# Gated linear attention in chunks of 64 tokens instead of 128, on one NeuronCore of Trainium2

## The chip, the core and the metric

The kernel runs on one NeuronCore of a Trainium2 chip. The metric is the device time of one execution in microseconds. Shown for a kernel are the median of several executions, and one further execution that the hardware profiler recorded.

## What is computed

One transformer block on 8192 tokens of width 512, in fp32. The part that matters here is the gated linear attention with 16 heads of 64 channels:

```python
h = layernorm(x) * (1 + ca) + sa
q, k, v = h @ Wq.T, h @ Wk.T, h @ Wv.T            # [s, 16, 64] each
g = -softplus(h @ Wd.T + bd)                      # [s, 16]
k = k * sigmoid(h @ Wg.T)
s_t = exp(g_t) * s_{t-1} + outer(k_t, v_t)        # per head, 64 x 64
o_t = q_t @ s_t
x = x + ga * ((rmsnorm(o) * norm_w * sigmoid(h @ Wog.T)) @ Wo.T)
```

After it comes a feed-forward part (three products of 512 x 512). The scan over 8192 tokens isn't made token by token: within a chunk of tokens the scores k.q, weighted by the decay between the two tokens and cut to the past, are multiplied with v, and what came before the chunk enters through the 64 x 64 state.

## The kernel before

`prepare` (L69) splits the attention's weights into high and low parts. `attention_pass` (L346) makes o and writes it to HBM. `output_pass` (L976) reads it back and makes the rest. Only the second of these is changed, and in `output_pass` the order in which o is loaded (`load_o`, L1030).

The tokens are cut into 32 tiles of 256 tokens (T), each of two chunks (NC) of 128 (CH). The pass is software-pipelined: in turn i the projections of tile i are made while the attention of tile i-1 is made. A turn has 8 pairs p of heads. Each engine has its program written out by hand, `pe_tile`, `act_tile`, `dve_tile`, `pool_tile` and `sp_tile`, and they meet only in semaphores. Turns 2 to 29 are a loop; 0, 1, 30, 31 and 32 are written out.

For pair p PE does, in this order (L571 to L638):
- two transposes of kg into psX (L581), from which DVE makes kw, the keys weighted by the decay to the chunk's end (L873);
- the projection g of the next tile (`project`, L509: 4 steps of k, each with 3 matmuls of 128 x 128 with 256 moving columns, L55 to L57);
- the attention's matmuls, called the block here: `weigh_v` (L540) with 4 matmuls v.prob of the pair before, 4 matmuls kw.v into psK (L606), 8 scores kg.q into psS (L614), and `add_held` (L552) with 4 matmuls of state.q of the pair before, which add to the sums of `weigh_v` in psO;
- the projections q and k of the next tile. Behind pair 4 come four projections of v; for p = 0 the projection v4 stands before the block and v5 behind it, and behind pair 7 stand g, q and k of the last channels.

All of the block is fp32. An fp32 matmul of the program is two instructions in the profile, and each has a weight load of its own on the row PEld. `weigh_v` and psK use half of the array (128 rows x 64 columns), the scores and `add_held` a quarter (64 x 64):

```python
nc.tensor.matmul(psO[side * DH:(side + 1) * DH, h, :], v[:, c, p * P + h * DH:p * P + (h + 1) * DH],
                 prob[:, p % 2, 2 * h + c, :], start=True, stop=False, tile_position=(0, side * DH))
```

DVE, for each pair: kw (L873), qg (L818), the two steps of the state, mid (L883) and state (L886), each with 64 columns, then the product of prob with the scores (L889, 512 columns), then `gate_k` (L804) for the projection k. Pair 4 adds `norm_stats`, pair 5 the two steps to softplus' input ahead of kw (L862, L866) and g_raw and `norm_x` behind, pair 6 the copy of cum_out (L904). At p = 0 four `rest_h` (L799) end the pair. ACT makes the four exponentials of the decay (L730, 128 columns each), the copy held of the state (L712), the tanh of the gate (L686), the copy of o out of psO (`copy_o`, L717) and the copy of q (L699). POOL cuts the decay rows to the past (`mask_rows`, L943). SP loads the rows (`spread_rows` L424, `grow_rows` L431), stores o (`store_o` L445) and stores cum_out once a turn (L484).

Where PE waits: ahead of `weigh_v` for prob, mid, held, qg and o; ahead of L606 for kw, state, and for q and v (L599 to L602); ahead of the projection k of pair 6 for w_new and o (L629, L631).

Of the kernel before, what the change touches and what calls it, by code (L numbers as in the profile page):

```python
# [23 lines left out]
P = 128  # L24
# [321 lines left out]
def attention_pass(nc, t, W, norm, h_parts, next_jobs, stage, h_next, h_loaded, wmod_v, x_v, o_v, h_v, cum_v, cum_b):  # L346
    with ExitStack() as ctx:
# [3 lines left out]
        def ps(name, shape):  # L351
# [8 lines left out]
        prob = sb("prob", [P, 2, 4, CH])  # L360
# [5 lines left out]
        mid = sb("mid", [P, 2, DH])  # L366
# [7 lines left out]
        w_new = sb("w_new", [P, 4, NC * H])  # L374
        w_cur = sb("w_cur", [P, 3, NC, H])
        w_all = sb("w_all", [P, NC, NP])
# [7 lines left out]
        psS, psX, psK = psB[:, :, 0:2, :], psB[:, 0, 2:4, :], psB[:, 1, 2:4, 0:DH]  # L384
# [4 lines left out]
        psC = psT[:, 1, NC * H:4 * NC * H]  # L389
# [3 lines left out]
                 "m_sum m_read m_out gate cur proj by_act k e mask score prob kT kw inc mid state held qg gla o zero")  # L393
# [29 lines left out]

        def spread_rows(sp, i, p):  # L424
# [24 lines left out]
        def sp_tile(sp, i, gla, proj, prep, opens=False):  # L449
            j = i - 1  # L450
            for p in range(NP):
# [12 lines left out]
                if p == 7 and proj:  # L464
                    sp.wait_ge(s["n_rows"], 16 * (i + 1))
# [43 lines left out]
        def project(i, kind, b, pe, turns_decay=False):  # L509
# [30 lines left out]
        def weigh_v(pe, n, p):  # L540
            pe.wait_ge(s["prob"], n + 1)
            pe.wait_ge(s["mid"], n + 1)
# [3 lines left out]
            for c in range(NC):  # L546
                for h in range(2):
                    side = (h + c) % 2
                    nc.tensor.matmul(psO[side * DH:(side + 1) * DH, h, :], v[:, c, p * P + h * DH:p * P + (h + 1) * DH],
                                     prob[:, p % 2, 2 * h + c, :], start=True, stop=False, tile_position=(0, side * DH))  # L550

        def add_held(pe, p):  # L552
            for c, s_in in enumerate((held, mid)):
                for h in range(2):
                    r, side = slice(h * DH, (h + 1) * DH), (h + c) % 2
                    last = nc.tensor.matmul(psO[side * DH:(side + 1) * DH, h, :], s_in[r, p % 2, :],  # L556
                                            qg[r, p % 2, c * CH:(c + 1) * CH], start=False, stop=True,
                                            tile_position=(h * DH, side * DH))
# [10 lines left out]
        def pe_tile(pe, i, gla, proj, prep, opens=False):  # L569
            j = i - 1  # L570
            for p in range(NP):  # L571
# [11 lines left out]
                if p == 6 and proj:  # L583
                    pe.wait_ge(s["g_raw"], i + 1)
                    pe.wait_ge(s["hT"], KD * (i + 2 if prep else i + 1))
                    for n3, m in enumerate(("upto", "after", "ones")):
                        last = nc.tensor.matmul(psC[:, n3 * NC * H:(n3 + 1) * NC * H], t[m][:, :], g_raw[:, :],
                                                start=True, stop=True)
                    last.then_inc(s["cum"], 1)
                if p == 0 and gla:  # L590
                    project(j, "v", 4, pe)
                if p > 0 and proj:
                    project(i, "g", p - 1, pe)
                if gla:
                    if p > 0 or not opens:
                        if p == 7 and proj:
                            pe.wait_ge(s["n_out"], i + 1)
                        weigh_v(pe, n - 1, (p - 1) % NP)
                    pe.wait_ge(s["kw"], n + 1)  # L599
                    hold(pe, s["state"], n)  # L600
                    pe.wait_ge(s["by_act"], act_done(j, ("q", p)))
                    pe.wait_ge(s["by_act"], act_done(j, ("v", 5 if p > 3 else 3)))  # L602
                    for c in range(NC):
                        for h in range(2):
                            r = slice(h * DH, (h + 1) * DH)
                            last = nc.tensor.matmul(psK[r, c, :], kw[:, c, r],  # L606
                                                    v[:, c, p * P + h * DH:p * P + (h + 1) * DH],
                                                    start=True, stop=True, tile_position=(0, h * DH))
# [9 lines left out]
                    if p > 0 or not opens:  # L618
# [22 lines left out]
        def _(pe):  # L641
# [9 lines left out]
            weigh_v(pe, NP * NT - 1, NP - 1)  # L651
# [49 lines left out]
        def turn_decay(act, i):  # L701
# [3 lines left out]
            nc.scalar.activation(w_new[:, 1:4, :], psC.rearrange("p (a b) -> p a b", a=3),  # L705
# [725 lines left out]
```

## Time and profile before

| | us |
|---|---|
| median of 3 runs (3398.72 to 3400.33) | 3399.99 |
| the profiled execution's own time | 3399.61 |
| its span, first to last instruction | 3397.7 |
| PE busy (share of the span) | 3343.4 (98%) |
| PE weight loads busy | 3067.8 (90%) |
| DVE busy | 1707.5 (50%) |
| ACT busy | 1350.8 (40%) |
| POOL busy | 435.0 (13%) |

The span is the stretch that the profile covers; 1.9 us of the execution's own time lie around it. The shares of busy time are means over stages that differ: the weights are prepared until about 60 us, the attention pass ends at about 2104 us, and the rest is the output pass. The length of a matmul in the trace is from its start to its modelled end, and matmuls overlap, so what a group of them costs is read from the distance of starts, not from their lengths. PE at 98% therefore doesn't say that PE can't be made faster.

### The profile page before, as it was taken

The page shows a single profiled execution, that of the slowest core. Times are in us where ns is not written, and L with a number is a line of the kernel's source. Part 1 is how long each engine was busy: PE and PEld are TensorE (multiplying, and loading weights), DVE is VectorE, ACT ScalarE, POOL GpSimd, SP SyncE. Part 2 cuts the span into 40 slices and gives each one's busy share as a digit, 9 for nine tenths or more (in the row PEclk, how much of TensorE's full clock was granted, in tenths as well). Part 3 has the DMA queues.
Part 4 walks back from the last instruction along what each step waited for, and adds up shares of the span by engine and source line. Part 5 has one row for each costly group of instructions (what it writes and reads, how often), then busy time and mean ns, then how long its engine had stood idle before and what let it go on. Part 6 is the DMA issues. An engine that isn't in the chain of part 4 may idle for free. (4 is left out here: it accounts for less than half of the span.)

```text
span 3397.7 us, 84855 instructions
## 1 busy us (share of the span) xinstructions
PE 3343.4 (98%) x31109; PEld 3067.8 (90%) x31109; DVE 1707.5 (50%) x3988; ACT 1350.8 (40%) x3584; POOL 435.0 (13%) x723
## 2 busy tenths in 40 slices
PE   7999999999999999999999997999999999999998
PEld 6999999999999999999999996889998899999887
DVE  6333333333333333333333334677667766766776
ACT  4444444444444444444444444333333333333332
POOL 0101100111111011011011102111111111211110
PEclk8999999999999999999999999999999999999999
DMA  5232322322322322322322325322233222232320
GB/s 205 90 108 76 102 98 77 109 88 86 106 82 89 106 80 92 105 78 93 105 75 93 102 69 171 94 74 81 79 84 89 74 74 74 79 82 78 92 77 25
DMA packets 233704, 309.17 MB, mean 91 GB/s; under 512 B 16016, under 2 KB 149152, under 8 KB 233648
## 3 DMA queue, kind: packets, MB, share of 16 engines
q1 hardware_dynamic: 231536, 304.20, 28.9%
q10 hardware_dynamic: 2112, 4.19, 0.4%
q8 instruction: 39, 0.64, 0.1%
q14 instruction: 17, 0.14, 0.0%
HBM read 223.40 MB, written 84.93 MB: 91 GB/s over the span
## 5 line engine op out<-in xcount | busy, mean ns | idle before, releaser
L730 ACT ACTIVATE prob<-cum_rows,w_cur 128x128 f32<-128x128 f32 x1024 | 327.8, 395 | 8.9 <-issue 5.2
L883 DVE SCALAR_TENSOR_TENSOR mid<-state,w_all,psB 128x64 f32<-128x64 f32 x256 | 71.9, 281 | 515.6 <-PE psB L614 515.6
L809 DVE SCALAR_TENSOR_TENSOR kg<-gate,psJ 128x256 f32<-128x256 f32 x256 | 107.9, 421 | 403.2 <-PE psJ L57 364.5
L55 PE MATMUL psJ<-h_hi,w_q_hi 128*128 128x256 f32 x1024 | 309.1, 302 | 0.0
L55 PE MATMUL psJ<-h_hi,w_g_hi 128*128 128x256 f32 x1024 | 305.6, 298 | 3.5 <-DVE h_lo L801 3.5
L55 PE MATMUL psG<-h_hi,w_og_hi 128*128 128x256 f32 x1024 | 287.7, 281 | 6.0 <-ACT og L1167 3.1
L55 PE MATMUL psJ<-h_hi,w_k_hi 128*128 128x256 f32 x1024 | 286.8, 280 | 0.7 <-ACT w_new L705 0.7
L56 PE MATMUL psJ<-h_lo,w_g_hi 128*128 128x256 f32 x1024 | 286.2, 280 | 0.0
L56 PE MATMUL psJ<-h_lo,w_q_hi 128*128 128x256 f32 x1024 | 285.7, 279 | 0.0
L57 PE MATMUL psJ<-h_hi,w_g_lo 128*128 128x256 f32 x1024 | 285.7, 279 | 0.0
L57 PE MATMUL psJ<-h_hi,w_q_lo 128*128 128x256 f32 x1024 | 285.4, 279 | 0.0
L56 PE MATMUL psG<-h_lo,w_og_hi 128*128 128x256 f32 x1024 | 284.8, 278 | 0.0
L57 PE MATMUL psG<-h_hi,w_og_lo 128*128 128x256 f32 x1024 | 284.7, 278 | 0.0
L57 PE MATMUL psJ<-h_hi,w_k_lo 128*128 128x256 f32 x1024 | 284.4, 278 | 0.0
L56 PE MATMUL psJ<-h_lo,w_k_hi 128*128 128x256 f32 x1024 | 283.8, 277 | 0.0
L55 PE MATMUL psJ<-w_v_hi,h_hi 128*128 128x264 f32 (+1 forms) x768 | 252.8, 329 | 0.6 <-DVE kg L809 0.6
L56 PE MATMUL psJ<-w_v_lo,h_hi 128*128 128x264 f32 (+1 forms) x768 | 246.3, 321 | 0.0
L57 PE MATMUL psJ<-w_v_hi,h_lo 128*128 128x264 f32 (+1 forms) x768 | 246.1, 320 | 0.0
L717 ACT COPY o<-psP 128x256 f32<-128x256 f32 x256 | 94.8, 370 | 351.3 <-PE psP L556 347.8
L55 PEld LDWEIGHTS psJ<-h_hi,w_q_hi 128*128 128x128 f32 x1024 | 193.3, 189 | 37.3 <-issue 37.3
L1167 ACT ACTIVATE og<-psG 128x512 f32<-128x512 f32 x128 | 76.5, 598 | 356.5 <-PE psG L57 356.5
L699 ACT COPY q<-psJ 128x256 f32<-128x256 f32 x256 | 95.3, 372 | 276.3 <-PE psJ L57 276.3
(231 smaller groups left out, 9551.2 us busy)
## 6 DMA issues: line engine op xcount, KB each, us to landing
cum_rows<-cum_dram SPq DMA_DIRECT2D x256, 256.0 KB, 3.9
grown<-cum_dram SPq DMA_DIRECT2D x256, 128.0 KB
o_dram<-o SPq DMA_DIRECT2D x256, 128.0 KB, 3.3
o_cols<-o_dram SPq DMA_DIRECT2D x128, 256.0 KB, 4.9
an_norm_x<-in_L_attn_x_dram SPq DMA_DIRECT2D x32, 512.0 KB, 5.4
h_dram<-h_hi SPq DMA_DIRECT2D x32, 512.0 KB, 2.7
h_dram<-h_lo SPq DMA_DIRECT2D x32, 512.0 KB, 4.2
h_hi<-h_dram SPq DMA_DIRECT2D x32, 512.0 KB, 4.0
```

The lines of the kernel that those rows point to most:

```text
L55: nc.tensor.matmul(out, w_hi, x_hi, start=first, stop=False)
L56: nc.tensor.matmul(out, w_hi, x_lo, start=False, stop=False)
L57: return nc.tensor.matmul(out, w_lo, x_hi, start=False, stop=last)
L699: nc.scalar.copy(q[:, b, :], psJ[USES.index(("q", b)) % 2][:, 0:T]).then_inc(s["by_act"], 1)
L717: nc.scalar.copy(o[:, p % 2, :, :], psO[:, :, :]).then_inc(s["o"], 1)
L730: last = nc.scalar.activation(prob[:, p % 2, 2 * h + c, :], cum_rows[:, p % 4, 2 * h + c, :], ACT.Exp, bias=w_cur[:, 0, c, 2 * p + h:2 * p ...
L809: nc.vector.scalar_tensor_tensor(out=kg[:, b, :], in0=gate[:, b % 2, :], scalar=1.0, in1=psJ[USES.index(("k", b)) % 2][:, 0:T], op0=ALU.ad ...
L883: nc.vector.scalar_tensor_tensor(out=mid[:, p % 2, :], in0=state[:, p, :], scalar=w_all[:, 0, p:p + 1], in1=psK[:, 0, :], op0=ALU.mult, op ...
L1167: nc.scalar.activation(og[:, n % 2, :, :], psG[n % 2][:, :].rearrange("p (b t) -> p b t", b=2), ACT.Sigmoid).then_inc(s["sg"], 1)
```

## The change

The chunk becomes 64 tokens: a tile of 256 tokens is now four chunks, indexed (c, b) with b the half of a 128-token piece. Every matmul of the block is a quarter of the array with 64 moving columns, 8 of each kind. The state takes four steps for each tile instead of two. The products of prob and v go to psO and those of the state and q to psH, in another part of the same PSUM tensor, and are added outside: ACT copies psH to o, and then DVE adds psO (`sum_o`). PE's waits for the whole block stand ahead of the last three matmuls of the projection before it.

```diff
+        mid = sb("mid", [P, 2, 3, DH])
+        w_new = sb("w_new", [P, 5, NC * H])
+        w_all = sb("w_all", [P, NC, 2, NP])
+        g_half = sb("g_half", [P, 2, NC * H])
+        later = sb("later", [P, DH])
-        psS, psX, psK = psB[:, :, 0:2, :], psB[:, 0, 2:4, :], psB[:, 1, 2:4, 0:DH]
+        psS, psX = psB[:, :, 0, :], psB[:, 0, 2:4, :]
+        psK = psB[:, :, 1, :].rearrange("p b (c d) -> p b c d", c=NC)
+        psH = psP[:, :, 3, :]
...
         def spread_rows(sp, i, p):
             hold(sp, s["e"], NP * i + p - 3)
-            sp.dma_start(cum_rows[:, p % 4, :, :].rearrange("p (h c) t -> p h (c t)", h=2),
-                         cum_b[i, 0, 2 * p:2 * p + 2, :].unsqueeze(0).to_broadcast([P, 2, T])
-                         ).then_inc(spread[p % 4], 16)
+            for b in range(2):
+                sp.dma_start(rows_of(p)[b * DH:(b + 1) * DH, :, :],
+                             cum_b[i, 0, 2 * p:2 * p + 2, b * CH:(b + 1) * CH].unsqueeze(0).to_broadcast([DH, 2, CH])
+                             ).then_inc(spread[p % 4], 16)
...
-                    sp.dma_start(cum_v[i], cum_out[:, :]).then_inc(s["n_rows"], 16)
+                    for b in range(2):
+                        sp.dma_start(cum_v[i, :, b, :, :], cum_out[:, b * DH:(b + 1) * DH]).then_inc(s["n_rows"], 16)
...
+                if ready and k == KD - 1:
+                    ready()
...
-        def weigh_v(pe, n, p):
+        def o_ready(pe, n):
             pe.wait_ge(s["prob"], n + 1)
-            pe.wait_ge(s["mid"], n + 1)
+            pe.wait_ge(s["mid"], 3 * (n + 1))
             pe.wait_ge(s["held"], n + 1)
             pe.wait_ge(s["qg"], n + 1)
             hold(pe, s["o"], n)
+
+        def kv_ready(pe, j, p):
+            n = NP * j + p
+            pe.wait_ge(s["kw"], n + 1)
+            hold(pe, s["state"], n)
+            pe.wait_ge(s["by_act"], act_done(j, ("q", p)))
+            pe.wait_ge(s["by_act"], act_done(j, ("v", 5 if p > 3 else 3)))
+
+        def weigh_v(pe, p):
+            for h in range(2):
+                for b in range(2):
+                    for c in range(NC):
+                        nc.tensor.matmul(psO[c * DH:(c + 1) * DH, b, h * DH:(h + 1) * DH],
+                                         v[b * DH:(b + 1) * DH, c, p * P + h * DH:p * P + (h + 1) * DH],
+                                         prob[b * DH:(b + 1) * DH, p % 2, 2 * h + c, :], start=True, stop=True,
+                                         tile_position=(b * DH, c * DH))
 
         def add_held(pe, p):
+            for b in range(2):
+                for c in range(NC):
+                    for h in range(2):
+                        r = slice(h * DH, (h + 1) * DH)
+                        s_in = mid[r, p % 2, 2 * c + b - 1, :] if c or b else held[r, p % 2, :]
+                        last = nc.tensor.matmul(psH[c * DH:(c + 1) * DH, h, b * DH:(b + 1) * DH], s_in,
+                                                qg[r, p % 2, c * CH + b * DH:c * CH + (b + 1) * DH], start=True, stop=True,
+                                                tile_position=(h * DH, c * DH))
             last.then_inc(s["gla"], 1)
...
+                def ready():
+                    if follows:
+                        if p == 7 and proj:
+                            pe.wait_ge(s["n_out"], i + 1)
+                        o_ready(pe, n - 1)
+                    kv_ready(pe, j, p)
+
+                if p == 0 and gla:
+                    project(j, "v", 4, pe, ready=ready)
+                elif proj and p > 0:
+                    project(i, "g", p - 1, pe, ready=ready if gla else None)
...
+                        for b in range(2):
+                            for h in range(2):
+                                r, rows = slice(h * DH, (h + 1) * DH), slice(b * DH, (b + 1) * DH)
+                                last = nc.tensor.matmul(psK[r, b, c, :], kw[rows, c, r],
+                                                        v[rows, c, p * P + h * DH:p * P + (h + 1) * DH],
+                                                        start=True, stop=True, tile_position=(b * DH, h * DH))
...
-                                last = nc.tensor.matmul(psS[rows, h, c, :], kg[r, p, c * CH + b * DH:c * CH + (b + 1) * DH],
-                                                        q[r, p, c * CH:(c + 1) * CH], start=True, stop=True,
-                                                        tile_position=(h * DH, b * DH))
+                                at = slice(c * CH + b * DH, c * CH + (b + 1) * DH)
+                                last = nc.tensor.matmul(psS[rows, h, c * DH:(c + 1) * DH], kg[r, p, at], q[r, p, at],
+                                                        start=True, stop=True, tile_position=(h * DH, b * DH))
...
         def copy_o(act, n, p, j):
             act.wait_ge(s["gla"], n + 1)
             hold(act, store[p % 2], 16 * (NP // 2 * j + p // 2))
-            nc.scalar.copy(o[:, p % 2, :, :], psO[:, :, :]).then_inc(s["o"], 1)
+            nc.scalar.copy(o[:, p % 2, :, :], psH).then_inc(s["o_part"], 1)
...
+        def sum_o(dve, n, p):
+            dve.wait_ge(s["o_part"], n + 1)
+            nc.vector.tensor_tensor(o[:, p % 2, :, :].rearrange("p h (b t) -> p h b t", b=2),
+                                    o[:, p % 2, :, :].rearrange("p h (b t) -> p h b t", b=2),
+                                    psO.rearrange("p b (h t) -> p h b t", h=2), ALU.add).then_inc(s["o"], 1)
...
+                    for m in range(4):
+                        c, b = m // 2, m % 2
+                        if m:
+                            dve.wait_ge(s["mid"], 3 * n + m)
+                        into, done = (mid[:, p % 2, m, :], s["mid"]) if m < 3 else (state[:, p, :], s["state"])
+                        nc.vector.scalar_tensor_tensor(out=into, in0=mid[:, p % 2, m - 1, :] if m else state[:, p, :],
+                                                       scalar=w_all[:, c, b, p:p + 1], in1=psK[:, b, c, :], op0=ALU.mult,
+                                                       op1=ALU.add).then_inc(done, 1)
                     dve.wait_ge(s["e"], n + 1)
+                    pr = prob[:, p % 2, :, :].rearrange("p (h c) t -> p h (c t)", h=2)
+                    nc.vector.tensor_tensor(pr, pr, psS, ALU.mult).then_inc(s["prob"], 1)
+                if gla and (p > 0 or not opens):
+                    sum_o(dve, n - 1, (p - 1) % NP)
...
+                    for b in range(2):
+                        rows = slice(b * DH, (b + 1) * DH)
+                        nc.vector.tensor_scalar(g_half[rows, b, :].rearrange("p (h c) -> p c h", c=NC), zt[rows, 0, :, :],
+                                                -1.0, None, ALU.mult)
...
+        def mask_rows(pool, i, p):
...
-            nc.gpsimd.affine_select(out=cum_rows[:, p % 4, :, :], in_=cum_rows[:, p % 4, :, :], compare_op=ALU.is_ge,
-                                    fill=fill, base=0, pattern=[[0, 4], [1, CH]],
-                                    channel_multiplier=-1).then_inc(s["mask"], 1)
+            rows = rows_of(p).rearrange("p h (c t) -> p h c t", c=NC)
+            nc.gpsimd.tensor_tensor(rows, rows, later[:, :].unsqueeze(1).unsqueeze(1).to_broadcast([P, 2, NC, DH]),
+                                    ALU.add).then_inc(s["mask"], 1)
```

Not shown: the masks are cut to blocks of 64 once at the start, the exponentials read 64 columns each, the decay's matmul with ones takes g_half with 64 columns, qg is written with its pieces in another order, and `load_o` of the output pass reads the same bytes with four DMAs as before.

## Rows read from the trace of the kernel before

**Rows 1.** View by stages: us, busy time of each engine, clock, DMA share, GB/s
```profile
101.00:2062.50 1961.50, 1959.29 (x22169) 1821.87 (x22170) 735.62 (x2105) 878.17 (x2679) 210.14 (x523) 1.00 0.28 93
2062.50:2104.00 41.50, 27.23 (x324) 19.98 (x322) 26.92 (x53) 24.00 (x57) 12.15 (x22) 0.95 0.65 214
2104.00:3397.70 1293.70, 1279.58 (x8064) 1153.70 (x8064) 889.00 (x1698) 410.28 (x769) 206.51 (x160) 0.99 0.28 77
```

**Rows 2.** Timeline of PE over one pair: start us, length us, instructions
```profile
1000.25 0.28 PE L56 MATMUL psJ<-h_lo,w_g_hi 128*128 128x256 f32 x1
1000.37 0.28 PE L57 MATMUL psJ<-h_hi,w_g_lo 128*128 128x256 f32 x1
1000.58 0.66 PE L549 MATMUL psP<-prob,v 128*64 128x128 f32 x8
1001.06 0.40 PE L606 MATMUL psB<-v,kw 128*64 128x64 f32 x8
1001.39 0.67 PE L614 MATMUL psB<-q,kg 64*64 64x128 f32 x16
1001.88 0.27 PE L556 MATMUL psP<-qg,held 64*64 64x128 f32 x1
1001.89 0.28 PE L556 MATMUL psP<-qg,mid 64*64 64x128 f32 x2
...
1002.00 0.28 PE L556 MATMUL psP<-qg,mid 64*64 64x128 f32 x2
...
1002.21 0.39 PE L55 MATMUL psJ<-h_hi,w_q_hi 128*128 128x256 f32 x1
1002.43 0.28 PE L56 MATMUL psJ<-h_lo,w_q_hi 128*128 128x256 f32 x1
```

**Rows 3.** Groups by form, 300 to 1700 us: busy us, mean ns, idle
```profile
L606 PE MATMUL psB<-v,kw 128*64 128x64 f32 x1432 | 71.8, 221 | 0.0
```

**Rows 4.** View of one line, PE's sequencer: ns min/median/max, first and last start
```profile
L45 PEldq ALU_OP  x2: 32/32/32, 1001.5 to 1001.8; - x2
...
L45 PEldq EVENT_SEMAPHORE  x1: 51/51/51, 2080.9 to 2080.9; - x1
...
L601 PEldq EVENT_SEMAPHORE  x1: 51/51/51, 2081.0 to 2081.0; - x1
```

**Rows 5.** Timeline of DVE, ACT and PE around the same pair
```profile
1002.13 0.28 DVE L883 SCALAR_TENSOR_TENSOR mid<-state,w_all,psB 128x64 f32<-128x64 f32 x1 [1.99 <-PE psB L614]
1002.45 0.28 DVE L886 SCALAR_TENSOR_TENSOR state<-mid,w_all,psB 128x64 f32<-128x64 f32 x1
...
1005.60 0.42 DVE L873 TENSOR_TENSOR kw<-psB,w_cur 128x256 f32<-128x256 f32 x1
...
1002.43 0.37 ACT L717 COPY o<-psP 128x256 f32<-128x256 f32 x1 [0.96 <-PE psP L556]
...
1006.34 0.28 PE L55 MATMUL psJ<-h_hi,w_g_hi 128*128 128x256 f32 x1
```

**Rows 6.** Timeline of DVE and PE at pair 1 of a tile
```profile
1050.35 0.42 DVE L873 TENSOR_TENSOR kw<-psB,w_cur 128x256 f32<-128x256 f32 x1
...
1050.62 0.28 PE L55 MATMUL psJ<-h_hi,w_g_hi 128*128 128x256 f32 x1
```

**Rows 7.** Timeline of DVE and PE at pair 5 of a tile
```profile
1018.20 0.42 DVE L873 TENSOR_TENSOR kw<-psB,w_cur 128x256 f32<-128x256 f32 x1
...
1018.38 0.28 PE L55 MATMUL psJ<-h_hi,w_g_hi 128*128 128x256 f32 x1
```

**Rows 8.** Timeline of PE at pair 6 of a tile
```profile
1025.74 0.66 PE L549 MATMUL psP<-prob,v 128*64 128x128 f32 x8
...
1028.89 0.28 PE L55 MATMUL psJ<-h_hi,w_k_hi 128*128 128x256 f32 x1
```

**Rows 9.** POOL's groups over the whole span, and SP's timeline at a tile's end
```profile
L1322 POOL TENSOR_TENSOR sq<-sq 128x256 f32<-128x256 f32 x32 | 33.9, 1061 | 2.5
...
1032.14 2.07 SPq L427 DMA_DIRECT2D cum_rows<-cum_dram  x4
```

More of the change, by code:

```diff
@@ L359, in attention_pass @@
         o = sb("o", [P, 2, NC, CH])
-        prob = sb("prob", [P, 2, 4, CH])
+        prob = sb("prob", [P, 2, 4, DH])
         g_raw = sb("g_raw", [P, NC * H])
@@ L388, in attention_pass @@
         psT = ps("psT", [P, KD, T])
-        psC = psT[:, 1, NC * H:4 * NC * H]
+        psH = psP[:, :, 3, :]
+        psC = psT[:, 1, NC * H:5 * NC * H]
         psM = psP[:, 1, 2, 0:KD]
         s = signals(nc, ctx, "a", "xT hT h_hi h_lo h_kept zb softin e1 l soft g_raw cum w_new n_turned n_out n_rows "
-                 "m_sum m_read m_out gate cur proj by_act k e mask score prob kT kw inc mid state held qg gla o zero")
+                 "m_sum m_read m_out gate cur proj by_act k e mask score prob kT kw inc mid state held qg gla o_part o zero")
         s.update(norm["s"])
@@ L506, in _, with project @@
             sp.wait_ge(s["h_kept"], 32 * NT)
-        def project(i, kind, b, pe, turns_decay=False):
+        def project(i, kind, b, pe, turns_decay=False, ready=None):
             u = USES.index((kind, b))
@@ L545, in weigh_v @@
             hold(pe, s["o"], n)
[L546 to L550, printed above, removed]
-        def add_held(pe, p):
[L553 to L558, printed above, removed]
+        def kv_ready(pe, j, p):
[12 more added lines that the diff above has]
+                                         tile_position=(b * DH, c * DH))
+        def add_held(pe, p):
+            for b in range(2):
[6 more added lines that the diff above has]
+                                                tile_position=(h * DH, c * DH))
             last.then_inc(s["gla"], 1)
@@ L585, in pe_tile @@
                     pe.wait_ge(s["hT"], KD * (i + 2 if prep else i + 1))
-                    for n3, m in enumerate(("upto", "after", "ones")):
-                        last = nc.tensor.matmul(psC[:, n3 * NC * H:(n3 + 1) * NC * H], t[m][:, :], g_raw[:, :],
-                                                start=True, stop=True)
-                    last.then_inc(s["cum"], 1)
[L590 to L593, printed above, removed]
@@ L594, in pe_tile @@
-                if gla:
-                    if p > 0 or not opens:
+                    for n3, m in enumerate(("upto", "after")):
+                        nc.tensor.matmul(psC[:, n3 * NC * H:(n3 + 1) * NC * H], t[m][:, :], g_raw[:, :],
+                                         start=True, stop=True)
+                    last = nc.tensor.matmul(psC[:, 2 * NC * H:4 * NC * H], t["ones"][:, :],
+                                            g_half[:, :, :].rearrange("p b n -> p (b n)"), start=True, stop=True)
@@ L596, in pe_tile @@
+                    last.then_inc(s["cum"], 1)
+                follows = p > 0 or not opens
+                def ready():
+                    if follows:
                         if p == 7 and proj:
                             pe.wait_ge(s["n_out"], i + 1)
[L598 to L602, printed above, removed]
@@ L603, in pe_tile @@
-                    for c in range(NC):
[L604 to L608, printed above, removed]
+                        o_ready(pe, n - 1)
+                    kv_ready(pe, j, p)
@@ L650, in _ @@
             turn_w(pe, NW - 1)
-            weigh_v(pe, NP * NT - 1, NP - 1)
+            o_ready(pe, NP * NT - 1)
+            weigh_v(pe, NP - 1)
             add_held(pe, NP - 1)
@@ L729, in act_tile @@
                         for h in range(2):
-                            last = nc.scalar.activation(prob[:, p % 2, 2 * h + c, :], cum_rows[:, p % 4, 2 * h + c, :], ACT.Exp,
+                            last = nc.scalar.activation(prob[:, p % 2, 2 * h + c, :], rows_of(p)[:, h, c * DH:(c + 1) * DH], ACT.Exp,
                                                         bias=w_cur[:, 0, c, 2 * p + h:2 * p + h + 1], scale=-1.0)
@@ L817, in grow_q @@
             hold(dve, s["gla"], n - 1)
[L818 to L819 removed]
+            nc.vector.tensor_tensor(qg[:, p % 2, :].rearrange("p (c b t) -> p c b t", b=2, c=NC),
+                                    q[:, p, :].rearrange("p (c b t) -> p c b t", b=2, c=NC), grown[:, p % 2, :].rearrange(
+                "p (b c t) -> p c b t", b=2, c=NC), ALU.mult).then_inc(s["qg"], 1)
         def weigh_mod(dve, m):
@@ L925, in _ @@
         def _(dve):
+            nc.vector.memset(g_half[:, :, :], 0.0)
+            nc.vector.memset(t["upto"][0:DH, DH:P], 0.0)
+            nc.vector.memset(t["after"][DH:P, 0:DH], 0.0)
+            for b in range(2):
+                rows = slice(b * DH, (b + 1) * DH)
+                nc.vector.tensor_scalar(later[rows, :], t["upto"][rows, rows], -1.0, -1.0e30, ALU.add, ALU.mult)
             nc.vector.memset(state[:, :, :], 0.0).then_inc(s["zero"], 1)
@@ L936, in _ @@
                 rest_w(dve, n)
+            sum_o(dve, NP * NT - 1, NP - 1)
         def rsqrt(pool, n):
@@ L1031, in load_o @@
             for h in range(2):
-                for side in range(2):
-                    c = (h + side) % 2
+                for c in range(NC):
                     sp.dma_start(o[h * DH:(h + 1) * DH, :, c * CH:(c + 1) * CH],
-                                 o_v[i, side * DH:(side + 1) * DH, :, h, :]).then_inc(s["ol"], 16)
+                                 o_v[i, c * DH:(c + 1) * DH, :, h, :]).then_inc(s["ol"], 16)
         def sp_tile(sp, i, att, ffn, prep):
```

58 lines of the change are left out of this document (26 added, 32 removed).

## The prediction, made before the result was known

> **What bounds the kernel now.** I read the stages first [rows 1]. From 101 to 2062.5 us, where the attention pass runs in its steady order, PE is busy 1959 of 1961.5 us at the full clock, while DVE is busy 736 us and ACT 878 us. The output pass (1294 us) runs code that doesn't change. So the change is worth what it takes off PE's stream in those 1961 us, less what it adds in waits there.
>
> The timeline of PE over one pair gives the block [rows 2]. Matmuls of the projections start 0.12 us apart (1000.25, 1000.37). Without the block the next would start at 1000.49, and the first of q that keeps the step of 0.12 stands at 1002.43, so the block costs 1002.43 - 0.12 - 1000.49 = 1.82 us. By its starts: 0.09 us until the first of `weigh_v` (1000.58), 0.48 for `weigh_v`, 0.33 for psK, 0.49 for the scores, 0.22 for `add_held` (two sets of four, 0.11 us apart: 1001.89 and 2.00), then 0.11 until the first of q (2.21) and 0.10 more than a usual step until the second. That is the sum again.
>
> The reader should see two more things there. Matmuls in different quarters start together: in `add_held` held, mid and the next start 0.01 us apart and the next such set 0.11 us later, which is the time of one matmul of 128 moving columns. And where the shape of the array changes there is a gap. psK has four sets of two. From the whole length of its eight, 0.40 us, less the 0.22 us of one [rows 2, 3], a set takes 0.18 / 3 = 0.06 us. Four make 0.23, yet 0.33 pass until the scores: 0.10 us go to the change from half to quarter, and 0.05 more into the scores (0.49 against 4 x 0.11). The entry into `weigh_v` has such a 0.05 too (0.48 against 0.43).
>
> **The block after.** 8 matmuls of each kind, two instructions each, are 64 instructions, in 16 sets of four if all four quarters run side by side. In the order written, each four consecutive matmuls do take the four quarters, with the two row halves in different banks. A set of 64 columns isn't in the trace in quarters. The half of 0.109 is 0.055, and psK's sets show 0.06; I take 0.058. So: entry 0.09 + 0.05, 16 x 0.058 = 0.93, exit 0.11 + 0.10: 1.28 us. The gain is 0.54 to 0.55 us: 0.20 in `weigh_v`, 0.20 in the scores, 0.15 from the change of shape that goes, 0.01 lost in `add_held`. PE is the bound for 31 tiles of 8 pairs: 248 x 0.545 = 135 us.
>
> **What can feed it.** 64 instructions and their 64 weight loads now have to be handed to the array in 0.93 us, 7 ns each. The trace before never asks for more than one in 14 ns. What it shows of PE's sequencer [rows 4]: the register step for the projection q runs at 1001.5, when the scores have just begun, so everything left of the block is queued (by the code 20 instructions of the scores and 16 of `add_held`), and 24 more pass until the next one at 1001.8: 0.3 to 0.4 us, no slower than 16 ns each. In the tile without projections the wait ahead of `weigh_v` stands at 2080.9 and the one behind its 16 instructions at 2081.0, at most 0.2 us apart, waits included. So the cost of handing out lies between about nothing and 16 ns. With 36 queued, 92 are left: at 10 ns they fit into the 0.93 us, at 14 ns the block takes some 1.65 us, at 16 ns as long as before. I take the fast end, since the burst at 2080.9 is nearest to it.
>
> Here a page speaks against the change. The trace has starts 0.01 us apart within a set [rows 2], but its mean over a set is 0.109 / 4 = 27 ns for each matmul. The Trainium skill, TensorE: Matmul & The Clock Gate, section Wait — 56ns, not 53.3ns?, says that start-to-start never drops below about 25 ns, however few the columns. By that floor 64 matmuls take an estimated 1.6 us. It is the last rival below. I weigh it low, because a floor on each start would forbid the steps of 0.01 us.
>
> **The moved waits.** The waits for the block now stand ahead of the last three matmuls of g (v4 at pair 0), and everything behind them on PE's sequencer is held. So kw has to be done some 0.2 us (two steps of the sequencer, by rows 4 0.1 us each, an estimate) before the tenth matmul.
> - An ordinary pair: kw ends at 1005.60 + 0.42 = 1006.02, the tenth matmul starts at 1006.34 [rows 5]. No stall.
> - Pair 1: DVE makes the four low parts of h first. kw ends at 1050.77, the tenth stands at 1050.62 [rows 6]: 0.35 us.
> - Pair 5: two steps for softplus come before kw, which ends at 1018.62; the tenth stands at 1018.38 [rows 7]: 0.43 us.
> - Pair 6: the projection k waits for o of the pair before, which DVE now completes. DVE starts its steps of the state 1.55 us after the block's start (1002.13 against 1000.58) [rows 2, 5]; the scores come earlier, so 1.0 us. Four steps of 0.32 [rows 5] make 2.27, the product with 256 columns 0.34 (an operation of 256 columns, kw, takes 0.42, of which about 0.08 overlaps), and `sum_o` as much: 2.95. ACT's copy (done at 1002.80 in rows 5, 2.2 after the block's start, now 0.5 earlier) isn't what it waits for. The first k stood 3.15 after the block's start [rows 8], now 2.6. With the sequencer's 0.2 PE stands still for some 0.5 us.
>
> Together 1.28 us for each of 31 tiles, 39 us; from below nothing, if the queued matmuls cover it, from above twice as much, if other pairs stall by 0.15 us each.
>
> **What costs nothing, and its cover.** DVE gets 0.64 us for two steps and 0.34 for `sum_o` in each pair, and saves some 0.3 on prob; it is busy 736 of 1961 us [rows 1]. ACT's exponentials get shorter. POOL's add of 256 columns may take 1.06 us (its like in the output pass) [rows 9], in a pair of some 5.7 us. SP issues a second DMA for each pair and five more at a tile's end, 2.07 / 4 = 0.52 us each [rows 9]: the first `grown` of the next tile goes out 2.6 us later. qg of pair 0 needs it, and PE waits for that qg a pair later, over 5 us on; without that cover it would be a stall at pair 1. The wait for `o` on SP comes later by 0.8 us and holds only loads for pairs ahead.
>
> The last tile, without projections, isn't bound by PE (27 of 41.5 us) [rows 1]. There DVE's 0.7 us more for each of 8 pairs lie partly on the path: +4 us. Masks at the start and the last `sum_o`: +1 us.
>
> **Sum**, against the profiled execution's 3399.6 us, which is 0.4 below the median of 3400.0: 3399.6 - 135 + 39 + 5 = 3308.6. I say 3308 us.
>
> **Rivals.**
> - *No stalls (12%).* The queue covers the moved waits: 3399.6 - 135 + 5 = 3270. For it: the engine works behind the sequencer by up to half the block. Against: nothing of the block can be queued while the sequencer stands at the wait.
> - *Handing out limits, but less than now (14%).* At 11 to 14 ns for each instruction the block takes 1.4 to 1.65 us: gain 45 to 104 us, less 44: 3340 to 3399.
> - *Slower, by a floor on matmuls (10%).* Place: the block. If no stretch can be faster on average than the 27 ns of now, 64 matmuls take 1.74 us, and with entry and exit 2.09 us, 0.27 more than before: +67 us + 44 = 3511. The point from which it decides: the block of now less entry and exit is 1.47 us, less 0.18 for the stalls (44 us over 248 pairs) 1.29, over 64: above 20 ns for each matmul the kernel gets slower. For it: no window of eight matmuls in the trace beats 27 ns. Against: that is just what 128 columns in four quarters need. The page's floor of about 25 ns would give 3475 us by the same sum, an estimate.
> - *It isn't what it says (4%).* The quarters don't overlap at 64 columns beyond two at a time, or the gain of the block is eaten whole by stalls: within 7 us of 3400.
>
> **How the numbers follow.** The forecast has 60%, with a range of its own of 3285 to 3335 (a set of 0.055 or 0.06 us moves it by 12 us, the stalls by 20). The range of 8 in 10 takes in the whole of the first rival, the forecast, and half of the second: 3265 to 3370. A measurement of this kernel can tell 0.2%, 7 us, from no change. Faster: 0.60 + 0.12 + 0.14 = 0.86; within 0.2%: 0.04; slower: 0.10.
>
> **What would show it.** PE's timeline: 64 instructions of 64 x 64 with 64 columns, the starts of the four kinds 0.23 us apart, one gap at the entry and none between psK and the scores. A distance of 0.4 us between the kinds would show the floor. The attention pass from 101 us to its last projection, 1961.5 us now [rows 1], should take some 1866 us (135 less, 39 more). In the waits: PE idle behind kw at pairs 1 and 5, and behind o at pair 6, each 0.3 to 0.5 us; if PE waits behind prob or `sum_o` in every pair, the path through DVE was underrated and the forecast is wrong upwards. The output pass should stay at 1294 us.

## The result, and the profile after

| | us |
|---|---|
| before, median of 4 runs beside it (3398.72 to 3404.54) | 3400.16 |
| after, median of 4 runs (3440.64 to 3452.34) | 3447.15 |
| ratio after / before | 1.0135 [1.0123, 1.0148] |
| span of the profiled execution | 3445.8 |

The kernel got slower by 1.35%. The forecast was 3308 us.

Out of the page of after: its first part, one row of the queues (packets, MB, share of 16 engines), and two groups (busy us, mean ns, idle before and what ended it):

```profile
span 3445.8 us, 99642 instructions
PE 3288.3 (95%) x37253; PEld 3015.9 (88%) x37253; DVE 1888.0 (55%) x4825; ACT 1308.6 (38%) x3584; POOL 463.8 (13%) x723
q8 instruction: 290, 4.75, 0.6%
L55 PE MATMUL psJ<-h_hi,w_g_hi 128*128 128x256 f32 x1024 | 320.9, 313 | 36.5 <-DVE qg L852 30.5
L55 PE MATMUL psJ<-h_hi,w_k_hi 128*128 128x256 f32 x1024 | 292.0, 285 | 12.4 <-DVE o L889 10.9
```

PE is busy 55 us less (3343.4 before), and the span is 48 us longer: PE stands still for 103 us more. The stages say where (us, busy time of PE, PEld, DVE, ACT and POOL, clock, DMA share, GB/s):

```profile
101.00:2100.00 1999.00, 1897.39 (x28031) 1759.55 (x28031) 906.41 (x2904) 832.36 (x2668) 237.76 (x523) 0.99 0.23 75
2152.00:3445.80 1293.80, 1278.81 (x8064) 1152.99 (x8064) 889.63 (x1698) 411.08 (x769) 206.80 (x160) 0.99 0.29 77
```

The output pass takes 1293.8 us, as before [rows 1]. In the attention pass PE was idle 2 of 1961 us; now it is idle 102 of 1999. The mean granted clock of that stretch is 0.99, before it was 1.00; what is behind this is told below the table of turns. PE's waits (us in total, times, longest):

```profile
PE psB L606 <- issue: 54.1, 26, 2.6
PE psJ L55 <- DVE qg L852: 30.5, 63, 0.5
PE psJ L55 <- DVE o L889: 10.9, 28, 0.4
```

The second and third are the moved waits, larger than forecast. (The profile puts the second down to qg; the sequencer's rows further down show that it is kw, the DVE step ahead of qg.) The first, the largest, was in nobody's list: 26 times PE stood up to 2.6 us where nothing that the profile shows was late. It is at the end of each turn. PE's timeline there (start us, us):

```profile
1060.42 0.28 PE L57 MATMUL psJ<-h_hi,w_k_lo 128*128 128x256 f32 x1
1062.97 0.41 PE L606 MATMUL psB<-c_ident,kg 128*128 128x128 f32 x2 [2.26 <-issue]
```

Between these two matmuls PE's sequencer is nearly all the time at one instruction, the branch back to the top of the loop over i, from 1058.59 to 1062.69 us. Its row (ns min/median/max, first and last start) of after, and then of before:

```profile
L678 PEldq COMPARE_BRANCH  x28: 83/3924/4373, 219.9 to 1966.7; - x28
```
```profile
L645 PEldq COMPARE_BRANCH  x28: 76/208/246, 221.1 to 1919.5; - x28
```

The same branch takes 3.9 us where it took 0.2 (the 83 ns is the last one, which isn't taken). It starts while PE still works through queued matmuls, so PE stands still for less than the branch takes. A turn of PE's loop has 1911 instructions in the trace of after (matmuls, weight loads and the sequencer's own) and 1519 in that of before. And the queue that brings code moved 290 packets of 16 KB, where before has this row:

```profile
q8 instruction: 39, 0.64, 0.1%
```

That is (290 - 39) / 28 = 9 packets in each turn. Before, 39 came in the whole execution: its loop's code isn't fetched again, and that of after is, every turn.

The block itself did what was forecast. PE's timeline of an ordinary pair:

```profile
1084.68 0.28 PE L56 MATMUL psJ<-h_lo,w_g_hi 128*128 128x256 f32 x1
1084.79 0.28 PE L57 MATMUL psJ<-h_hi,w_g_lo 128*128 128x256 f32 x1
1085.06 0.36 PE L55 MATMUL psJ<-h_hi,w_g_hi 128*128 128x256 f32 x1
1085.25 0.28 PE L56 MATMUL psJ<-h_lo,w_g_hi 128*128 128x256 f32 x1
1085.37 0.28 PE L57 MATMUL psJ<-h_hi,w_g_lo 128*128 128x256 f32 x1
1085.58 0.46 PE L570 MATMUL psP<-prob,v 64*64 64x64 f32 x16
1085.86 0.41 PE L639 MATMUL psB<-v,kw 64*64 64x64 f32 x16
1086.10 0.41 PE L648 MATMUL psB<-q,kg 64*64 64x64 f32 x16
1086.33 0.22 PE L581 MATMUL psP<-qg,held 64*64 64x64 f32 x1
...
1086.67 0.38 PE L55 MATMUL psJ<-h_hi,w_q_hi 128*128 128x256 f32 x1
1086.89 0.28 PE L56 MATMUL psJ<-h_lo,w_q_hi 128*128 128x256 f32 x1
```

By the rule used for before, the block costs 1086.89 - 0.12 - (1085.37 + 0.12) = 1.28 us. The kinds start 0.28, 0.24 and 0.23 us apart; four sets in 0.23 are 0.058 each. But the tenth matmul of g (1085.06) starts 0.27 us after the ninth instead of 0.12. Here is what held it, first on DVE, then on PE's sequencer between 1084.4 and 1085.2 us:

```profile
1084.19 0.42 DVE L914 TENSOR_TENSOR kw<-psB,w_cur 128x256 f32<-128x256 f32 x1
```
```profile
L561 PEldq EVENT_SEMAPHORE  x1: 51/51/51, 1084.6 to 1084.6; - x1
...
L45 PEldq EVENT_SEMAPHORE  x1: 51/51/51, 1084.8 to 1084.8; - x1
...
L563 PEldq ALU_OP  x1: 36/36/36, 1084.9 to 1084.9; - x1
...
L564 PEldq EVENT_SEMAPHORE  x1: 51/51/51, 1085.0 to 1085.0; - x1
```

kw ends at 1084.61. The first row is PE's wait for kw, 0.03 us behind that. Three steps more stand behind it (state, a register step, `by_act`), 0.1 us each, and then the matmul: 0.45 us from kw, not 0.2.

Since the same stretches come back in every turn, I measured each turn by them, from the first matmul of a group to the first of the next, as a mean over the 30 turns that are alike (us; a block here goes from its first start to the first start of q, 1.63 before and 1.10 after, without the 0.09 ahead of it and the 0.10 in q):

| in a turn | before | after | difference |
|---|---|---|---|
| the 8 blocks | 13.05 | 8.80 | -4.25 |
| last k, and v4 (the branch is between) | 4.28 | 6.72 | +2.44 |
| g of pairs 1 and 5 | 3.12 | 4.66 | +1.54 |
| g of pairs 2, 3, 4 and 7 | 6.35 | 7.27 | +0.92 |
| q and k of pair 6 | 3.03 | 3.66 | +0.63 |
| all else | 33.04 | 33.34 | +0.30 |
| turn | 62.88 | 64.44 | +1.56 |

Times 31 that is 48 us, the distance of the two spans. (The branch back is taken 27 times. Its cost is spread here over 30 turns, so it is multiplied by 30 below.)

The second row of the table holds two costs. The last k is longer by 2.04 us (3.40 against 1.36): there PE stands still. v4 is longer by 0.40 us (3.32 against 2.92), and there PE works, but at a lower clock. In 8 of the 30 turns the granted clock fell to half, TensorE's level of 1.2 GHz, between 0.7 us before and 1.0 us after PE took up work again behind the branch; in the attention pass it stood there for 27 us in all. In these turns v4 takes 4.38 us, in the other 22 it takes 2.94. One of each, in the view by windows (the clock stands behind POOL's count, 0.62 and 1.00):

```profile
1385.78:1390.31 4.53, 4.53 (x14) 3.30 (x12) 0.85 (x2) 0.00 (x0) 0.21 (x1) 0.62 0.26 71
1451.53:1454.47 2.94, 2.94 (x14) 2.15 (x13) 0.60 (x2) 0.00 (x0) 0.22 (x1) 1.00 0.29 81
```

Ahead of both PE had stood still, for 2.30 and 1.96 us. In the kernel before, no v4 of the 30 runs at half clock. The last k, with its gap, takes 3.48 to 4.14 us ahead of the turns that are hit, and 3.03 to 3.91 us ahead of the others behind a long branch: the longer gaps are hit more often, but what decides it for one turn stays open.

### The profile page after: what moved, and what is told of

It is laid out like the page before. It is cut to its first block and busy times, and to the rows that moved or that the text cites. A ratio compares the mean times of both kernels' runs of the same rounds, so it can differ in the third digit from the quotient of the medians.

```text
span 3445.8 us, 99642 instructions
## 1 busy us (share of the span) xinstructions
PE 3288.3 (95%) x37253; PEld 3015.9 (88%) x37253; DVE 1888.0 (55%) x4825; ACT 1308.6 (38%) x3584; POOL 463.8 (13%) x723
## 5 line engine op out<-in xcount | busy, mean ns | idle before, releaser
L55 PE MATMUL psJ<-h_hi,w_g_hi 128*128 128x256 f32 x1024 | 320.9, 313 | 36.5 <-DVE qg L852 30.5
L764 ACT ACTIVATE prob<-cum_rows,w_cur 128x64 f32<-128x64 f32 x1024 | 273.6, 344 | 8.7 <-issue 4.9
L55 PEld LDWEIGHTS psJ<-h_hi,w_g_hi 128*128 128x128 f32 x1024 | 193.2, 189 | 72.8 <-issue 56.6
L720 ACT ACTIVATE gate<-psJ 128x256 f32<-128x256 f32 x256 | 98.5, 385 | 359.3 <-PE psJ L57 357.9
```

Source lines behind the costliest of these rows:

```text
L55: nc.tensor.matmul(out, w_hi, x_hi, start=first, stop=False)
L720: nc.scalar.activation(gate[:, b % 2, :], psJ[USES.index(("g", b)) % 2][:, 0:T], ACT.Tanh, scale=0.5).then_inc(s["by_act"], 1)
L764: last = nc.scalar.activation(prob[:, p % 2, 2 * h + c, :], rows_of(p)[:, h, c * DH:(c + 1) * DH], ACT.Exp, bias=w_cur[:, 0, c, 2 * p + h: ...
```

## The experiments

Two theories stood for what the trace shows. **A:** the branch costs because the turn's code has grown beyond what the sequencer keeps. **C:** PE's waits ahead of the last three matmuls of a projection stand too early, and cost what stands behind kw and o. The rivals: **B**, the gap at a turn's end is some late semaphore and not code; and the early waits are needed, since they let the block's 128 instructions and loads be handed out while matmuls still run. (The letters are those of the expectations; D and E come with the last three runs.)

### PE's turns written out: e1_unrolled, and the same on the kernel before: e2_before_unrolled

```diff
-            with pe.Fori(2, NT - 2) as i:
+            for i in range(2, NT - 2):
```

> The changed kernel with the turns 2 to 29 of PE's program written out one after the other, PE alone; the other engines keep their loops. Theory A (the backward branch of PE's loop waits about 3.9 us for code that is no longer held, because a turn has grown from 1519 to 1911 of PE's instructions): the gap of 2.2 us behind the last projection k of each turn goes, and so does the slower start of v4: 28 x 2.4 = 67 us less, about 3380 us, below the kernel before. Theory B (the gap at the turn's end is PE waiting for the products of prob or for kg of the last pair): it stays, and the time stays at 3447 within 10 us. If code can't be streamed fast enough in a straight line either, the gaps move elsewhere and the time stays too.

> The kernel before with the same turns of PE written out. Theory A: its branch took 0.2 us and was hidden, so nothing is gained: 3400 us within 5. Theory B and any theory by which writing out helps whatever the length of the turn: faster by tens of us as well.

Without the loop after takes 3372.41 us (3367.63 to 3376.96), 75 less, ratio 0.9917 [0.99, 0.9933] to before. The control takes 3406.32, 1.0014 [1.0004, 1.0024]: writing turns out gains before nothing. In e1's turn the last k takes 1.39 us, where after has 3.40 and before 1.36, and v4 2.93 (after 3.32). So the gap belongs to the branch, and with what follows it, it is worth what the table says (2.44 x 30 = 73): 61 us of PE standing still and 12 us of v4 at half clock. In e1 no v4 runs at half clock. Fetching code doesn't cost by itself: e1's instruction queue moves 242 packets and e2's 193, and PE doesn't stand for them. It stands where a branch goes back to code that has to be fetched.

### Is it the length of the turn? e5_before_1775, e6_before_1903, e11_before_1647

These leave the change out altogether. The kernel before gets idle scores in front of its own (they are overwritten and reach no result), in all pairs (1775 instructions in a turn), twice in half of the pairs (1903), or once in half of them (1647):

```diff
+                    for c in range(NC if p in range(NP) else 0):
+                        for b in range(2):
+                            for h in range(2):
...
+                                nc.tensor.matmul(psS[rows, h, c, 0:DH], kg[...], q[r, p, c * CH:c * CH + DH], ...)
```

> The kernel before, loop kept, with its scores of 64 columns made once more in each pair ahead of the true ones, as filling: 8 matmuls, 32 instructions a pair, so that a turn of PE's loop has 1775 instructions instead of 1519. The product is overwritten at once and nothing that is computed changes. The filling itself costs four sets of 0.058 us a pair, 0.23 x 248 = 58 us. The reading is the length of PE's branch at the turn's end. If about 1900 instructions are the point from which code is fetched anew (theory A with a limit near 2048 less what is read ahead), it stays at 0.2 us and the time is 3458 us; if the limit lies lower, it is 3 to 4 us and the time some 3510 us.

> The same with the filling twice in the pairs 0, 2, 4 and 6: a turn has 1903 instructions, about the 1911 of the changed kernel. The filling costs 12 x 0.23 x 31 = 87 us. Theory A (length alone makes the branch wait): the branch takes about 3.9 us, 2.4 us a turn are lost in the gap behind it and in v4, and the time is 3400 + 87 + 67 = 3554 us. If something else of the change makes the branch wait (its DMAs on SP, its other code), the branch stays at 0.2 us and the time is 3487 us.

> The kernel before, loop kept, with the filling (scores of 64 columns made once more) in the pairs 0, 2, 4 and 6 alone: a turn has 1647 instructions, between the 1519 at which the branch took 0.2 us and the 1775 at which it took 4.3. The filling costs 4 x 0.23 x 31 = 29 us. If the limit lies above 1647, the branch stays at 0.2 us and the time is 3430 us; if below, the branch takes about 4 us and the time is some 3500 us. I expect the first, since 1647 with one block of instructions ahead is still under 2048.

They took 3558.16, 3576.78 and 3543.45 us (1.0464, 1.0518 and 1.0419 of before), each more than I had expected even for a long branch. The branch's rows, one of each kernel in this order:

```profile
L652 PEldq COMPARE_BRANCH  x28: 83/4334/4892, 225.0 to 2078.4; - x28
```
```profile
L659 PEldq COMPARE_BRANCH  x28: 83/4154/4664, 228.2 to 2077.3; - x28
```
```profile
L652 PEldq COMPARE_BRANCH  x28: 83/4182/4752, 225.0 to 2058.1; - x28
```

All three have it, with the waits, DVE and all else as in before. The third was to show a short branch and did not: the limit lies below 1647 instructions, and not below the 1520 of e8, further down. (Whether it also depends on where the loop lies in the code wasn't tested.) The filling costs 0.233 us a pair (the block goes from 1.634 to 1.868), in e5 8 x 31 x 0.233 = 58 us; the last k and v4 grow by 3.42 us a turn, x 30 = 103 us. That is 161, and 157 were measured. In e11 filling (29) and branch (3.65 x 30 = 110) make 139 of 142. In e6 they make 87 + 75 = 162 of 176; but its two executions took 3564.50 and 3589.07 us, at mean granted clocks of 0.993 and 0.986. The trace is of the first, 164 us above before, and a clock lower by 0.007 over 3589 us is the 25 us between the two.

The clock also explains most of why similar branches cost from 2.44 to 3.65 us a turn. v4 runs at half clock in 24 of 30 turns in e11, in 16 in e5, in 8 in after and in 2 in e6, and takes 4.4 to 4.5 us there against 2.93 or 2.94 in the others. In before, e1, e2, e4, e7, e8, e9 and e10, where the branch is short or isn't there, no v4 does.

### The waits: e8_before_waits_ahead, e3_one_ahead, e4_unrolled_waits_back

e8 gives the kernel before nothing of the change but the waits ahead of the last three matmuls of g or v4. Its turn has 1520 instructions. In `project`:

```diff
...
+                if ready and k == KD - 1:
+                    ready()
...
```

> The kernel before, with this one part of the change alone: PE's waits for the block ahead of the last three matmuls of the projection. Theory C says that their place costs, whatever DVE does behind them: g becomes 0.22 us longer in the pairs 2, 3, 4 and 7 and about 0.75 in pairs 1 and 5, 2.4 us a turn less what the shorter entry into the block gives back: 3400 + 75 = 3475 us. If it is DVE's four steps and its sum that make kw late in the changed kernel, the waits cost nothing here: 3400 us.

Measured 3471.78 us, 1.021 [1.0193, 1.0227]: 71 us slower, with the same old block. Per turn g of pairs 1 and 5 takes 1.51 us more, g of the others 0.89: after's table to within 0.03. So what DVE has to do for 64-token chunks isn't behind these stalls. Its branch is as in before:

```profile
L655 PEldq COMPARE_BRANCH  x28: 76/208/246, 225.9 to 1984.4; - x28
```

e3 keeps after and its loop, and puts `ready()` ahead of the last matmul of the three only.

> The changed kernel, loop kept, PE's waits for the block ahead of the last one instead of the last three matmuls of the projection. Theory C (the waits stand too early: kw is ready about 0.5 us before PE's sequencer has worked through what stands behind it, and the rest of g is held meanwhile): the stall in g falls from 0.22 us to about nothing in four pairs of a turn and from 0.75 to some 0.5 in pairs 1 and 5, 1.3 us for each of 31 turns, 3447 - 42 = 3405 us. Its rival (the stalls in g come from DVE being late, so that the wait ends when it ends): the stall only moves by two matmuls and the time stays within 10 us of 3447.

It takes 3418.49, 1.0052 [1.0036, 1.0069]. The stalls of ordinary pairs are gone (6.34 us for g, before 6.35), those of pairs 1 and 5 fall from 1.54 to 1.04. It gives back 0.5 us at v4 (3.82 us against after's 3.32), and that is the clock: v4 runs at half clock in 17 turns of e3 (4.50 us) and at full clock in 13 (2.93). I had expected 3405; 0.5 x 30 = 15 us accounts for the 13 that e3 takes more.

e4 is e1 with the waits where before has them: for o behind g and ahead of `weigh_v`, for kw behind `weigh_v`.

```diff
...
-                    project(i, "g", p - 1, pe, ready=ready if gla else None)
...
+                        o_ready(pe, n - 1)
                         weigh_v(pe, (p - 1) % NP)
+                    kv_ready(pe, j, p)
```

> The changed kernel with PE's turns written out and its waits where they were before the change: those for prob, mid, held, qg and o behind the projection and ahead of the products of prob and v, those for kw, state, q and v ahead of kw.v. Theories A and C together: 67 us less for the branch and 2.4 us less for each of 31 turns (75 us) for the stalls in g, about 3305 us; the block of 1.28 us stays as it is. If the early waits are needed to keep the array fed through the block (the reason one could have for moving them), the block grows instead and the time stays near that of the written-out kernel, 3380 us.

3293.36 us (3290.76 to 3294.33), 0.9686 [0.967, 0.9703]: 79 us less than e1. The stalls of g are gone (6.27, and 1.58 and 1.59 at pairs 1 and 5), and the block stays at 1.1 us by starts (8.79 for the eight, after 8.80). So handing out needs no head start, and the waits ahead bought nothing. (Waits back with the loop kept wasn't measured; by the branch's 2.44 us it would take some 73 us more than e4, an estimate.)

### What is left: e7_wait_of_k_later, e10_grown_earlier, e9_grown_earlier_k_later

In e4 PE still stands at pair 6, where k waits for o (theory D). e7 moves that wait, with the transpose of the decay that stands behind k's first step, to k's last step. e10 (theory E) is e4 with one thing changed on SP: the `grown` of the next tile's pairs 0 and 1 goes out right behind its own row of cum_rows, not behind all eight. e9 has both.

```diff
-                if k == 0 and turns_decay:
+                if k == KD - 1 and turns_decay:
+                    turns_decay()
...
```
```diff
-                    for pair in range(2):
-                        grow_rows(sp, i, pair)
+                        if pair < 2:
+                            grow_rows(sp, i, pair)
```

> The changed kernel with PE's turns written out and its waits back as in the run of 3293 us, and in pair 6 the waits for w_new and o, with the transpose that needs them, moved from ahead of the projection k to its last step, nine matmuls later. Theory D (in pair 6 PE stands 0.4 us for sum_o): the gap behind q of pair 6 goes, 0.4 us for each of 31 turns, 3293 - 13 = 3280 us. If w_new or the transposed rows are wanted sooner (the rows of the next tile are stored from them), the stall appears at the turn's end instead and nothing is gained.

> The kernel of 3293 us (turns written out, waits back) with the same order on SP and nothing else. There the gap ahead of pair 1 is smaller (0.12 us and 0.2 behind it, on average), so theory E gives 10 us: 3285 us; if SP's order doesn't matter, 3293 us.

> The kernel of 3302 us (turns written out, waits back, the waits of pair 6 later) and on SP the rows `grown` of the pairs 0 and 1 issued each behind its `cum_rows` instead of behind all eight of them. Theory E (with two DMAs a pair the first `grown` of a tile goes out last and lands 6 us after the tile's start; qg of pair 0 waits for it, DVE's steps of the state, prob and the four low parts of h queue behind that qg, and PE stands ahead of pair 1): the gap of 0.6 to 3 us between the transposes of x and pair 1's goes, 0.8 us a turn on average and what it drags along, and the saving of pair 6 shows: 3275 us within 7. If the gap comes from somewhere else, the time stays at 3302.

e7: 3302.31 us, 0.9708 [0.9692, 0.9724], 9 us more than e4 where 13 less were expected (the two intervals just overlap). The stall of pair 6 went (3.49 to 2.96 us), but the transposes at pair 1 took 2.34 us instead of 1.50. In five of the 30 turns they took 3.5 us or more, and in four of these the clock fell to half there too. The four last 62.3 us, the other 26 last 59.3, and e4's mean is 59.25: the four carry the loss. DVE's group of qg, e7 and then e9 (idle before, and what ended it):

```profile
L845 DVE TENSOR_TENSOR qg<-q,grown 128x256 f32<-128x256 f32 x256 | 120.2, 470 | 176.8 <-DMA grown<-cum_dram 163.0 <-issue 9.3 <-ACT v L702 4.4
```
```profile
L845 DVE TENSOR_TENSOR qg<-q,grown 128x256 f32<-128x256 f32 x256 | 114.4, 447 | 12.6 <-DMA grown<-cum_dram 12.2 <-issue 0.3
```

In e7 DVE stood 163 us for `grown`: moving PE's wait ahead of cum's transpose later made the rows leave later, and the DMA is the second half of that path. e10 alone gives 3288.73, 0.9667 [0.9651, 0.9683], 5 us less than e4 and not clear of the spread; the two together 3269.15 (3267.2 to 3271.46), 0.9607 [0.9591, 0.9623]. With `grown` early, the later wait of k is worth 20 us; without, it costs 9. This kernel is 3.9% faster than before and 5.2% faster than after.

## Why the prediction was wrong

**The block: right.** 1.82 to 1.28 us was forecast and 1.28 measured, 135 us forecast for the pass and 4.25 x 31 = 132 measured. **Handing out** at the fast end was right: 64 matmuls start in 0.93 us, 14.5 ns each, with their 64 loads. So the rival that handing out limits fell, and so did "Slower, by a floor on matmuls". The Trainium skill (TensorE: Matmul & The Clock Gate, section Wait — 56ns, not 53.3ns?) says that "Start-to-start never drops below ≈25 ns however small N is". Over matmuls that lie in different quarters this doesn't hold here. Within one quarter the starts are 58 ns apart, and of that these runs say nothing.

**What failed first: a term that wasn't in the sum, under "What can feed it".** Each pair gets 24 matmuls and 24 weight loads more (64 instead of 40 in the block), 384 of the 392 instructions by which the turn grew. I only asked whether they can be handed out, never what they do to the loop that holds them. The branch takes 3.9 us, and 2.44 us are lost for it in a turn's mean, 73 us in all: 61 us in which PE stands still, and 12 us in which v4 behind it runs at half clock, which wasn't in the sum either. e1, e2 and e5 show it, from both sides. The Trainium skill (Runtime: NRT & Kernel Launch, section Instruction fetch mechanics) has the mechanism: PE's instruction memory holds 2048 instructions and is a FIFO, filled in blocks of 256, and a taken branch to code outside "the current 2-page window" waits for a fetch. The runs agree that a branch to code no longer held waits for a fetch, but not on the point from which it does: a turn of 1520 instructions, six blocks and not two, still branches back in 0.2 us, and one of 1647, still under 2048, doesn't. If two blocks are always under way ahead, 2048 - 2 x 256 = 1536 would be the limit; that is an estimate from the page's figures, and nothing here tests it closer.

**What failed second: the size of the moved waits.** The mechanism was as forecast, kw and o arriving late. The term "kw has to be done some 0.2 us (two steps of the sequencer, ...)" before the tenth matmul should have counted what stands behind that wait in `ready`: state, the register step and `by_act`, four steps with the wait itself, 0.45 us at an ordinary pair. At pair 1:

```profile
1072.19 0.42 DVE L914 TENSOR_TENSOR kw<-psB,w_cur 128x256 f32<-128x256 f32 x1
```
```profile
1072.35 0.28 PE L57 MATMUL psJ<-h_hi,w_g_lo 128*128 128x256 f32 x1
1073.15 0.36 PE L55 MATMUL psJ<-h_hi,w_g_hi 128*128 128x256 f32 x1 [0.53 <-DVE qg L852]
```

kw ends at 1072.61, the tenth matmul comes 0.54 us later. With 0.25 to 0.34 us more everywhere, "An ordinary pair: no stall" turned into 0.23 us (0.92 over four pairs), and pairs 1 and 5 into 0.76 and 0.78 instead of 0.35 and 0.43. Pair 6's 0.5 was right in kind and size (0.63). In all 3.09 us a turn instead of 1.28, 96 us instead of 39; above even my upper bound of twice 39. e8 gives 71 us for g's part alone, and e4 takes 79 back.

The sum, with what was measured: -132 + 73 + 96 + 9 (the 0.30 of all else, whose cause is left open) = +46; the medians stand 47 apart. Each failure alone would have left the kernel faster: e1, with the stalls and no branch, takes 3372, and the forecast with the branch and nothing else wrong would be 3308 + 73 = 3381, an estimate. Both together turn the sign.

**The rivals.** "Slower" had the right sign by the wrong mechanism: nothing in the block decides. "No stalls" at 3270 is what e9 reaches (3269), but with four more edits than the change has: turns written out, waits back, k's wait later, `grown` earlier.

**"Costs nothing": right in after, wrong once PE is faster.** POOL's add is 737 ns in the profile (bound 1.06), DVE's steps for o end 2.90 us after the block's start (forecast 2.95). SP's later `grown` was covered in after, where no stall behind it shows at pair 1's transposes (1.19 us, as before). In after DVE's qg waits 54 us for it in all (10 before), in e4 120 us and in e7 163, and the transposes at pair 1 take 1.50 and 2.34 us.

## What to carry to other kernels

When a change adds instructions to a loop on PE, count the instructions of one turn before and after, and look at the row of its branch and at the instruction queue's packets: a loop that no longer fits pays at every turn, and writing the turns out was the cure here. Look at the granted clock behind a gap as well: part of a gap's price can lie in the work that follows it. When a wait moves ahead of queued work, count every semaphore and register step behind it on the sequencer, at 0.1 us each on PE here, not only the distance to the producer. And once the first bound gives way, a step that "costs nothing" has to be read again: the same later wait of k loses 9 us with the old order of SP's DMAs (e7 against e4) and gains 20 with the new one (e9 against e10).

## What the runs showed of the hardware that I had not expected

- PE's branch back over 1519 or 1520 instructions takes 0.2 us (median 208 ns), over 1647, 1775, 1903 and 1911 it takes 3.9 to 4.3 (medians), with no growth along that row. The other engines' branches stay at 45 to 56 ns in both kernels.
- Four quarter matmuls of 64 x 64 with 64 columns take 58 ns: one instruction each 14.5 ns on average, sustained over 64 of them, weight loads included.
- Behind a long branch (gaps of some 2 us on PE) the granted clock fell to half in 8 of 30 turns of after, 17 in e3, 16 in e5, 24 in e11 and 2 in e6, and v4 there took 4.4 to 4.5 us instead of 2.93. In e8, whose 71 us of stalls are spread in pieces of 0.2 to 0.8 us, no v4 was hit.
